# Two attention layers with heads of 8: value products on packed weights, two copies in place of one, and fewer waits of TensorE

## What is computed

```python
x = _layernorm(x + _L0_attn_ref(x, ...))             # 16 heads of 8, no mask
x = _layernorm(x + _L0_xattn_ref(x, ctx_1024, ...))  # 16 heads of 8, causal
x = _layernorm(x + _L0_ffn_ref(x, ...))
x = _layernorm(x + _L1_attn_ref(x, ...))             # 16 heads of 64
x = _layernorm(x + _L1_xattn_ref(ctx_1024, x, ...))
x = _layernorm(x + _L1_ffn_ref(x, ...))              # experts
```

```python
out = softmax(q @ k.T / sqrt(8)) @ v   # for each of the 16 heads, columns 8h to 8h+7
out = out.reshape(64, 128) @ Wo + bo
```

## Time and profile before

| | us |
|---|---|
| median of 3 runs | 1567.57 (1566.75 to 1570.45) |
| profiled execution | 1571.52 |
| span of its instructions | 1569.8 |
| self and cross stage within the span | 0 to 279 |

### The profile page before, as it was taken

The page is one execution under the profiler, slowest core; times in us unless marked ns, Lnnn a source line. Parts: engine busy times, 40 slices in busy tenths (PEclk is TensorE's granted clock), DMA queues, the critical chain, the costliest instruction groups (busy, mean ns, idle before and its releaser), DMA issues. The chain is left out here.

```text
span 1569.8 us, 80230 instructions
## 1 busy us (share of the span) xinstructions
PE 1506.7 (96%) x32004; PEld 1283.2 (82%) x32004; DVE 1207.5 (77%) x3446; ACT 912.9 (58%) x2620; POOL 692.9 (44%) x1140
## 2 busy tenths in 40 slices
PE   7998999999999999999999999999999999999795
PEld 5887887887777778788788776899999999999564
DVE  7998888686777777777777775688888888888664
ACT  5887888534545555555555554666666666666251
POOL 4789777212333333333333332344444444444346
PEclk9999999999999999999999999999999999999998
DMA  4215222112210001011110010212122121212331
GB/s 114 70 55 147 68 65 63 48 53 61 66 36 27 27 27 30 27 27 31 29 30 27 27 28 26 55 48 65 53 56 62 47 64 45 66 44 63 99 103 32
DMA packets 157680, 82.72 MB, mean 53 GB/s; under 512 B 17641, under 2 KB 153115, under 8 KB 157568
## 3 DMA queue, kind: packets, MB, share of 16 engines
q1 hardware_dynamic: 154800, 77.68, 18.0%
q0 software_dynamic: 2048, 3.15, 0.6%
q10 hardware_dynamic: 720, 0.33, 0.1%
HBM read 61.03 MB, written 21.27 MB: 52 GB/s over the span
## 5 line engine op out<-in xcount | busy, mean ns | idle before, releaser
L1528 PE MATMUL bank<-diff_xT,diff_w_score 128*32 128x128 f32 x8192 | 249.3, 273 | 1.8 <-DVE diff_z L1761 1.1
L1528 PEld LDWEIGHTS bank<-diff_xT,diff_w_score 128*32 128x32 f32 x8192 | 219.0, 110 | 28.7 <-issue 15.4
L1656 ACT ACTIVATE diff_keys<-bank 128x512 f32<-128x512 f32 x256 | 152.5, 596 | 149.6 <-PE bank L1528 149.6
L2135 ACT ACTIVATE lat_prob<-bank,lat_neg_max 128x128 f32<-128x128 f32 x512 | 180.7, 367 | 78.9 <-DVE lat_neg_max L2290 77.8
L1846 POOL TENSOR_TENSOR diff_prob<-diff_prob,diff_inv_sum 128x512 f32<-128x512 f32 x64 | 67.1, 1049 | 338.6 <-DVE diff_inv_sum L1749 338.6
L2352 POOL TENSOR_TENSOR lat_prob<-lat_prob,lat_inv_sum 128x512 f32<-128x512 f32 x128 | 133.4, 1042 | 146.9 <-DVE lat_inv_sum L2272 146.0
L2026 PE MATMUL bank<-lat_catT,lat_w_score 128*128 128x128 f32 x1024 | 137.9, 278 | 3.4 <-issue 2.7
L2058 PE MATMUL bank<-lat_catT,lat_query 128*128 128x128 f32 x1024 | 138.4, 278 | 2.3 <-ACT lat_query L2146 2.1
L2046 PE MATMUL bank<-lat_w_vo,lat_ctxT 128*128 128x128 f32 x1024 | 130.3, 275 | 1.1 <-ACT lat_ctxT L2158 1.1
L2026 PEld LDWEIGHTS bank<-lat_catT,lat_w_score 128*128 128x128 f32 x1024 | 124.4, 192 | 5.0 <-issue 4.1
L2058 PEld LDWEIGHTS bank<-lat_catT,lat_query 128*128 128x128 f32 x1024 | 124.5, 192 | 4.7 <-ACT lat_query L2146 3.7
(11 more groups left out here) (275 smaller groups left out, 3589.8 us busy)
## 6 DMA issues: line engine op xcount, KB each, us to landing
lat_c_rep<-cat SPq DMA_DIRECT2D x128, 128.0 KB
stage<-low_y SPq DMA_DIRECT2D x64, 64.0 KB, 1.6
diff_x_rep<-stage SPq DMA_DIRECT2D x128, 32.0 KB, 1.7
lat_c_t<-cat SPq DMA_DIRECT2D x32, 128.0 KB, 2.1
exp_w<-in_L_ffn_w_dram SPq DMA_DIRECT2D x16, 256.0 KB
expert_rows<-latw_zeros SPq DMA_DIRECT2D x4, 548.0 KB
exp_rows<-expert_rows SPq DMA_DIRECT2D x8, 274.0 KB
low_x_t<-in_x_dram SPq DMA_DIRECT2D x32, 64.0 KB, 1.8
```

Of the source, the lines that this page charges most:

```text
L1528: last = nc.tensor.matmul(ring[(k + d) % 2][at, j * P:(j + 1) * P], w_score[:, H1 * (k // 2) + HS * d + 4 * (k % 2) + j, at], xT[:, :], st ...
L1656: nc.scalar.activation(keys[:, k // 2, 4 * (k % 2):4 * (k % 2) + 4, :].rearrange("p h t -> p (h t)"), ring[(k + d) % 2][:, :], ACT.Copy).t ...
L2135: last = nc.scalar.activation(prob[:, q, m, :], ps_s[q][:, m * T:(m + 1) * T], ACT.Exp, bias=neg_max[:, q, m:m + 1], accum_out=row_sum[:, ...
```

## The change

- `wv` holds, for even and for odd heads, only the 64 columns of these heads, packed. The value product becomes 8 matmuls of 64 columns, and `ps_v` takes 128 columns in place of 256.
- ScalarE's copy into `v_blk` becomes two: partitions 0 to 63 into the even heads' columns, partitions 64 to 127 into the odd heads'. `v_ready` counts two for each pair. The columns that are not written stay zero from a memset of the whole `v_blk` at the start; the memset of `wv` is gone, and the copies that pack the weights write without gaps.
- In a slot in the middle of the run TensorE has seven waits fewer: `onorm_done`, `oT_ready` and the first `pT_ready` ahead of the probability-value product, `xT_ready` and `pT_ready` ahead of the transposes of the inputs, `xT_ready` and `qT_ready` ahead of the key product. In the first and last slots some of them stay.

```diff
-        self.wv = sb("wv", [P, 2, 2, P])
+        self.wv = sb("wv", [P, 2, 2, S])
...
-                        last = nc.tensor.matmul(ps_v[L * n:L * (n + 1), b * P:(b + 1) * P],
+                        last = nc.tensor.matmul(ps_v[L * n:L * (n + 1), b * S:(b + 1) * S],
...
-                wait(pe, self.onorm_done, i - 2)
-                wait(pe, self.oT_ready, i - 2)
...
-                    if hp % 4 == 0:
+                    if hp == 4 or hp == 0 and not on(0):
                         wait(pe, self.pT_ready, 2 * i - 3 + hp // 4)
...
                 wait(pe, self.x_loaded[par], 32 * (k + 2) - 8 * NPAIR if cross else 16 * (k + 2))
-                wait(pe, self.xT_ready, i + 2)
-                wait(pe, self.pT_ready, 2 * i - 2)
+                if isinstance(i, int) and i < 2:
+                    wait(pe, self.xT_ready, i + 2)
...
-                wait(pe, self.xT_ready, i + 2)
-                wait(pe, self.qT_ready, i + 1)
+                if isinstance(i, int) and i < 2:
+                    wait(pe, self.xT_ready, i + 2)
...
-                wait(pe, self.v_ready, i + 1 if on(0) else NI)
+                wait(pe, self.v_ready, 2 * i + 2 if on(0) else 2 * NI)
...
-                nc.scalar.activation(self.v_blk[:, 1 - par, :, :, 0:2 * HD0],
-                                     ps_v[:, 0:2 * P].rearrange("p (b g e) -> p b g e", b=2, e=2 * HD0),
-                                     ACT.Copy).then_inc(self.v_ready, 1)
+                for odd in range(2):
+                    at = slice(odd * S, (odd + 1) * S)
+                    nc.scalar.activation(self.v_blk[at, 1 - par, :, :, odd * HD0:(odd + 1) * HD0],
+                                         ps_v[at, 0:P].rearrange("p (b g e) -> p b g e", b=2, e=HD0),
+                                         ACT.Copy).then_inc(self.v_ready, 1)
...
-                    self.wv[:, w, odd, :].rearrange("p (g o e) -> p g o e", o=2, e=HD0)[:, :, odd, :],
+                    self.wv[:, w, odd, :].rearrange("p (g e) -> p g e", e=HD0),
...
-        nc.vector.memset(self.wv[:, :, :, :], 0.0).then_inc(self.wv_zeroed, 1)
         both = self.v_blk[:, :, :, :, :].rearrange("p n b g e -> p (n b g) e")
-        nc.vector.memset(both[:, :, 2 * HD0:VW], 0.0).then_inc(self.ones_done, 1)
+        nc.vector.memset(both, 0.0).then_inc(self.ones_done, 1)
```

4 lines of the change are left out of this document (1 added, 3 removed).

## The result

The changed kernel takes 1573.71 us (median of 10 runs, 1571.96 to 1577.97) against 1569.18 (1563.86 to 1571.16) for the kernel before on the same chip: ratio 1.0033, 95% interval 1.0022 to 1.0044. It is slower by a third of a percent. The forecast was 0.45% faster, and the measured time lies above the range. The profiled execution is one of 1571.96 us with a span of 1570.3.

The account below looks back on a forecast made before the run. Bound: TensorE's cross-slot loop, closed by ScalarE's probabilities copy, with VectorE next in the self stage. Cross 5.1 + self 1.5 + start 0.4 = 7.0 us off the 1567.57 median gives 1560.6 us, 0.45% less; range 1556.5 to 1566.5.

Parts of the forecast that it names:

- Value product, 0.427 to 0.213: TensorE's four passes per column group, at 64 columns instead of 128, take 0.213 us less in each slot.
- rival (c): Instructions, not columns, set the value product's time; gain about 1 us, total 1566.5 us; chance 0.12.
- The cross loop gives all of it back, 3.80: Cross stage: TensorE's loop falls from 4.01 to 3.80 us over 24 regular slots, 5.1 us in all.
- VectorE stops the self stage at 3.58 with a branch slot of 3.86: Self stage: VectorE's shortest slot is 3.58 us, though TensorE alone would reach 3.47; each fourth slot takes 3.86.
- Rival (b): VectorE does not stop the self stage and the waits give 0.09 a cross slot; total 1555.3 us; chance 0.08.
- the self term: Self stage: 0.07 us less a slot over 22 slots, 1.5 us in all.
- Two halves: 0.34, that is 0.06 more: ScalarE's two half copies of values block 0.34 us against 0.28 for one; bounds 0.06 and 0.28 more.
- The 0.06 is hidden: ScalarE has 0.24 us spare in the self slot, so the extra copy time costs nothing; uncovered it would cost 3 us.
- rival (a): The second probabilities copy or another ScalarE step takes the loop's place; gain 3.7 us, total 1563.9 us; chance 0.17.
- Bounds 0 and 3 x 0.03 = 0.09 a slot; I take 0: TensorE: removing the seven long-met waits gains between 0 and 0.09 us a slot, counted as 0.
- The eight cross slots: 0, at most 1.7: Cross slots in 128 to 168 us wait for GpSimd and transfers; gain counted as 0, at most 1.7 us.
- Start, 0.4: First two value products, run while TensorE is slow, save 0.4 us, between 0 and 0.85.

Follow-up runs that it names:

- one copy: Changed kernel with one ScalarE copy of 128 partitions and 128 columns instead of two, odd heads' placing left out: ratio 1.0027 to the kernel before.
- the reversed kernel: Changed kernel with its two half copies in reverse order, partitions 64 to 127 first: ratio 1.0033 to the kernel before.
- the second profile: Profile from running the unaltered changed kernel again, on one chip with three variants: ratio 1.0030 to the kernel before.
- the kernel of the waits alone: Kernel before without the seven waits, nothing else changed: ratio 1.0046 to the kernel before.
- the other pairs: Without the waits against with fillers or waits: waits alone and its filler, 0.40%; changed kernel and its filler, 0.44%; changed kernel and waits back, 0.52%.

## Why the prediction was wrong

- **Value product, 0.427 to 0.213: right.** 0.46 to 0.25 in every regular slot. So the columns set it, and rival (c) is out, for matmuls spread over four column groups.
- **The cross loop gives all of it back, 3.80, and VectorE stops the self stage at 3.58 with a branch slot of 3.86: right as mechanisms**, and hidden in the changed kernel. With one copy or the reverse order the slots are 3.80 and 3.60 (3.87 at the branch), and VectorE's instructions follow one another through the whole self slot of the reversed kernel, 3.60 from one subtraction of the row maxima (96.63) to the next (100.23). Rival (b) is out. But the self term was too large even so: the slot beside the branch slot takes 3.73, so four slots take 3.60 + 3.73 + 3.87 + 3.60 = 14.80, where the sum had 14.60 and the kernel before takes 14.88 (3.68, 3.68, 3.84, 3.68). That is 0.02 a slot in place of 0.07. The sum had let the slot beside a late one run short; it runs long.
- **"Two halves: 0.34, that is 0.06 more", "a half blocks as long as the whole" as the upper bound: the step that failed on ScalarE.** The 0.17 came from copies that all start at partition 0. The two halves cost 0.60 up to the next instruction, 0.32 more than the one copy, above my upper bound of 0.28, and the instruction after that 0.14 more again: 0.46 in all, against 0.24 of room. "The 0.06 is hidden" fell with it. This is rival (a) in its second form, another ScalarE step; it cost 0.06 in a cross slot (24 x 0.06 = 1.4 us) and turned the self stage from the forecast 0.07 less to 0.05 more a slot (22 x 0.12 = 2.6, of which the hold has 22 x 0.07 = 1.5 by the kernels without it, and the term just named the rest). I had looked for a shortage at the second copy of the probabilities; it came at the copy of the transposed input, earlier in ScalarE's slot.
- **"Bounds 0 and 3 x 0.03 = 0.09 a slot; I take 0", for the seven waits: right for the loops once they run, wrong for the program. This is the step that failed on TensorE, and the larger of the two.** Steady slots are the same to 0.01 with and without them. But the sum had no term for TensorE's instruction stream, and I took below zero as excluded: it was +0.46% alone, some 7 us, as large as the whole forecast gain and of the other sign.
- **"The eight cross slots: 0, at most 1.7":** wrong for the same reason. I read their gaps as GpSimd's and transfers' and did not ask what moves where TensorE's own code is being loaded. From the 32nd to the 40th value product they took 37.0 us before and 38.4 after, and the one behind them, which the sum had among the 24, 4.01 before and 5.74 after.
- **Start, 0.4:** the second value product does come 0.42 earlier after the first (3.67 for 4.09), but by the tenth value product the changed kernel was 0.6 later. With the waits back it was 1.1 earlier.
- **Rival (d), the clock:** not as it was put, by a wait for VectorE, and not as the first cause. But the granted clock did fall, to 0.96 in the stretch from 128 to 168 us (0.92 in the second profile), behind the pauses for code, and cost about 1.4 us in the slot of the longest one (the estimate above). The kernel of the waits alone loses as much with the clock at 1.00 throughout the 12 slots.

With the measured terms: 24 x 0.15 = 3.6 less in the cross stage, 22 x 0.05 = 1.1 more in the self stage, and about 7 more from the code: 4.5 slower, as measured. That close a match is luck: the intervals of the ratios are 2 us wide to each side, and the price of the waits is 6 to 8 us by the other pairs (0.40, 0.44 and 0.52%). The first two terms alone, 2.5 less, are 0.16%; the changed kernel with its waits back measured 0.19%.

## What to carry to other kernels

A wait that others imply is not free to remove at the end of tuning: it is an instruction, and where code runs for the first time, written out or in a loop's first pass, its removal shifts where the engine runs out of loaded instructions. Compare with a filler in its place before crediting or blaming the edit, and distrust any gain under half a percent that has not been seen at two code positions. When an operation is cut by partitions, put the part that starts elsewhere where the engine waits anyway, and read the spacing from instructions that change their start partition, not from ones that all start at 0.

## What the hardware showed that I had not expected

- ScalarE holds an instruction whose start partition differs from the last one's until all before have finished: 0.30 from a 128-column half copy to the half that starts elsewhere, 0.30 (0.60 less 0.30) on to the exponential where that one changes back, 0.18 (0.48 less 0.30) where it does not, and 0.66 instead of 0.52 to the next copy. The order of two halves alone decides how many are held.
- TensorE stops for up to 2.5 us in the middle of matmuls that wait for nothing, at the same matmuls in two executions, always at the same place in a block of 256 instructions and 1.2 to 1.8 us after a 16 KB packet of its code. In the attention stages it does so only where code runs for the first time, at a DMA share of 0.57 (the seven slots of the changed kernel) and at 0.26 (the five) alike; from a loop's second pass on it does not.
- Three more instructions in a slot of 245, in the places of the seven waits, made the kernel 0.40 to 0.63% faster, whatever they waited for. 47 more ahead of all slots cost 0.4 us at the first value product (10.27 to 10.66) and yet the kernels with them measured 0.03% to 0.39% faster, those without the seven by the most (0.13 to 0.39%); with the seven it is at most 0.11%, within the intervals.
